# Softplus as one activation, down products split on GpSimd, three banks for up products: a two-layer kernel on one core

## The chip, the cores and the metric

The kernel runs on one core of a Trainium2 chip. The metric is device time in microseconds (us) for one execution. Engines are named as in the profile: PE (TensorE matrix products), PEld (its weight loads), DVE (VectorE), ACT (ScalarE), POOL (GpSimd), SP (SyncE, which only issues DMAs here).

## What is computed

The input is 32 sequences of 256 rows of 128 channels. Two layers follow each other, each of the form x + s(x̂) * silu(f(x̂)), where x̂ is the row-normalised x. The change touches the second layer, cut here to what matters:

```python
# s: a selective scan
xr = x @ W_in;  x_in, res = xr[..., :256], xr[..., 256:]
xc = silu(depthwise_causal_conv4(x_in) + conv_b)
p = xc @ W_x
delta = softplus(p[..., :16] @ W_dt + b_dt)        # log(1 + exp(.))
h = h * d_t + B_t * x_t;  y_t = h.sum(axis=1) * C_t
s = (y * silu(res)) @ W_out
# f: experts, 2 shared and 16 routed, 64 wide each
shared = gelu(x @ up_s) @ down_s
gate = softmax(x @ router_w.T), all but the four largest set to 0
routed = (gelu(x @ up_r) * gate) @ down_r
f = shared + routed
```

The first layer is a recurrent mixing of another kind with a three-layer network of sign weights; nothing of it is changed but how its code is written out.

## The kernel before

The 8192 rows are 16 groups of 512, turned so that channels lie on the 128 partitions and the group's rows along the free dimension: nearly every tile is 128x512. All of x stays in SBUF. The first layer runs over the 16 groups, then the second. The order of work is written out by hand, one queue per engine, with semaphores between them; nothing reorders it. Each engine's body for group step n works on three groups at once: f = n (front part), m = n - 1 (scan and down products), t = n - 2 (the last product, and the sum into x). Loops over n repeat the body; in the second layer the body comes twice in the loop, since buffers alternate.

What matters in a step of the second layer:

- The 18 experts are 9 chunks of 128 (chunk 0 is shared, 1 to 8 are routed). An **up product** (`expert_in(c)`, PE, L1177) is a split product: both factors are halved into two float16 parts, and three float16 products are summed in PSUM (high x high, high x low, low x high). It goes to one of two PSUM banks by turns. ACT takes the Gelu of it (`gelu(c)`, L662).
- A routed chunk is then multiplied by the gate: chunks 1 to 3 by POOL (L444), chunks 4 to 8 by DVE (`gated`, L1046), one step later. The **down product** (`expert_out(c)`) is one float32 product per chunk; all nine are summed in one bank.
- The gate comes from the router: Exp on ACT (L692), top four on DVE (L1009 to L1025), the spread over partitions on POOL (L434), four transposes on PE (L1419) and an evacuation by ACT (`gates_out`, L599) behind the last Gelu.
- softplus is Exp on ACT (L641), a cap on DVE (L1057), Ln on ACT (L645) and a maximum with the input on DVE (L1061).
- The scan input is L1077, the scan L1087, its output product L1094, all on DVE. `output_weight` (L1068) takes the product of output weights out of PSUM and multiplies it by the residual's Silu; `low_xc` (L1073) is the low half of the convolved input.
- The convolution is six DVE instructions (L1034) on PSUM. Row statistics are L726 and L731 on DVE, the row spread L366 and L368 on POOL, the normalising L753 on DVE.
- ACT loads another set of function tables three times a step: for Silu (L707), Exp and Ln (L685), Gelu (L697).
- The group's last steps: Silu of the experts' sum (`ffn_silu`, L604) on ACT, its product with the scan's output on DVE (L1104), transposes, and the sum into x (L1150).

## Time and profile before

| | us |
|---|---|
| median of 3 runs | 686.22 (683.71 to 689.05) |
| the profiled execution | 683.87 |
| its span, first to last instruction | 682.1 |
| PE busy | 630.9 (93%) |
| DVE busy | 630.7 (92%) |
| ACT busy | 506.7 (74%) |
| POOL busy | 280.0 (41%) |

The span is what lies between the first and the last instruction; 1.8 us lie around it. The first layer takes some 270 us of it, the second the rest. The granted clock of PE is 1.00 in every slice (2.4 GHz), but for the last at 0.96. DMA is idle but for the weights at the start and a load or store of 256 KB per group. Names: many tiles of the second layer are cut from one buffer and appear as `arena`; the PSUM banks appear as `bank`. One float32 product of 512 columns is two records. A record's length has a part that overlaps the next instruction, so the sum over a row of instructions goes by their starts. Instructions on the same line of a helper are told apart by their tiles.

### The profile page before, as it was taken

The numbers are of one execution on the slowest core, as the hardware profiler recorded it, in microseconds if no ns is written. First come the engines' busy times: TensorE is split into PE (matmuls) and PEld (weight loads), VectorE is DVE, ScalarE is ACT, GpSimd is POOL, SyncE is SP. The second block draws the span as 40 slices with busy tenths as digits, with TensorE's granted clock in tenths as the row PEclk, the third lists the DMA queues.
The fourth block names the chain that finished last, engine by engine and source line by source line (L and its number), as shares of the span: only waits on it lengthen the run. The fifth ranks groups of instructions, "written<-read, shape, count | busy, mean of one in ns | idle before, by whom it ended". The sixth has DMA issues, their size and how long they took to land. (4 is left out here: it accounts for less than half of the span.)

```text
span 682.1 us, 10868 instructions
## 1 busy us (share of the span) xinstructions
PE 630.9 (93%) x2714; PEld 301.5 (44%) x2714; DVE 630.7 (92%) x1470; ACT 506.7 (74%) x808; POOL 280.0 (41%) x275
## 2 busy tenths in 40 slices
PE   4779999999999997889999999999999999999985
PEld 2334444444444443444444444444444444444442
DVE  4999999999999999989999999999999999999866
ACT  2846666666666665887887888888789788888874
POOL 6557777777676765133122212303303221230220
PEclk9999999999999999999999999999999999999999
DMA  7331000000000000000000000000000000000000
GB/s 174 106 94 31 0 1 0 0 0 0 0 0 0 0 0 0 1 1 0 17 17 0 16 15 0 16 15 0 15 15 15 0 15 15 0 15 15 0 16 31
DMA packets 10739, 11.29 MB, mean 17 GB/s; under 512 B 4800, under 2 KB 6288, under 8 KB 10720
## 3 DMA queue, kind: packets, MB, share of 16 engines
q1 hardware_dynamic: 9744, 10.73, 5.3%
q0 software_dynamic: 112, 0.33, 0.1%
q8 instruction: 8, 0.13, 0.1%
q10 hardware_dynamic: 864, 0.00, 0.1%
q14 instruction: 11, 0.09, 0.0%
HBM read 6.87 MB, written 4.19 MB: 16 GB/s over the span
## 5 line engine op out<-in xcount | busy, mean ns | idle before, releaser
L1177 PE MATMUL bank<-arena,w 128*128 128x512 f16 x640 | 148.6, 379 | 4.0 <-DVE arena L788 4.0
L1177 PE MATMUL bank<-arena,dnT 128*128 128x512 f32 x288 | 138.6, 592 | 0.0
L662 ACT ACTIVATE arena<-bank,xinv 128x512 f32<-128x512 f32 x144 | 94.8, 688 | 37.7 <-PE bank L1177 37.5
L444 POOL TENSOR_TENSOR arena<-arena 128x512 f32<-128x512 f32 x48 | 59.7, 1273 | 135.5 <-ACT arena L599 135.5
L1177 PEld LDWEIGHTS bank<-arena,w 128*128 128x128 f16 x640 | 62.5, 98 | 78.2 <-issue 10.0
L491 ACT ACTIVATE arena<-bank 128x512 f16<-128x512 f32 x96 | 53.9, 607 | 35.6 <-PE bank L1177 35.6
L434 POOL TENSOR_TENSOR arena<-arena 128x512 f32<-128x512 f32 x16 | 16.8, 1051 | 151.6 <-DVE arena L1025 151.6
L1177 PEld LDWEIGHTS bank<-arena,dnT 128*128 128x128 f32 x288 | 53.7, 191 | 35.9 <-issue 21.2
L1177 PE MATMUL bank<-arena,wsqT 128*128 128x512 f32 x128 | 64.5, 608 | 4.7 <-DVE arena L797 4.7
L1034 DVE SCALAR_TENSOR_TENSOR arena<-bank,cws,arena 128x506 f32<-128x506 f32 (+1 forms) x96 | 67.0, 740 | 1.1
L788 DVE SCALAR_TENSOR_TENSOR arena<-bank,arena 128x512 f16<-128x512 f32 x96 | 60.2, 670 | 2.4 <-ACT arena L491 1.2
L1046 DVE TENSOR_TENSOR arena<-arena 128x512 f32<-128x512 f32 x80 | 52.3, 686 | 0.0
L409 POOL TENSOR_TENSOR arena<-arena 128x512 f16<-128x512 f32 x32 | 36.9, 1156 | 18.0 <-ACT arena L491 18.0
L413 POOL TENSOR_TENSOR arena<-arena 128x512 f32<-128x512 f32 x16 | 20.3, 1271 | 48.1 <-DVE arena L835 45.2
L488 ACT ACTIVATE arena<-bank 128x512 f32<-128x512 f32 x32 | 19.1, 597 | 27.1 <-PE bank L1177 27.1
L1087 DVE TENSOR_TENSOR_SCAN arena<-arena 128x256 f32<-128x256 f32 x64 | 38.9, 668 | 0.0
L368 POOL TENSOR_TENSOR rstd<-ve,neghalf 128x4 f32<-128x4 f32 x32 | 37.2, 1164 | 2.5
L1177 PE MATMUL bank<-arena,wcH 128*128 128x512 f16 x128 | 38.1, 379 | 0.0
L637 ACT ACTIVATE arena<-arena 128x512 f32<-128x512 f32 x32 | 20.2, 631 | 18.8 <-DVE arena L1034 18.8
L1177 PEld LDWEIGHTS bank<-arena,wsqT 128*128 128x128 f32 x128 | 24.6, 195 | 21.5 <-issue 9.1
L1177 PE MATMUL bank<-xh,upH 128*128 128x512 f16 x72 | 27.3, 380 | 6.3 <-ACT arena L662 4.6
L1177 PE MATMUL bank<-arena,w_out 128*128 128x512 f32 x64 | 30.2, 594 | 3.1 <-DVE arena L1094 3.1
(223 smaller groups left out, 1497.7 us busy)
## 6 DMA issues: line engine op xcount, KB each, us to landing
x_all<-in_L_attn_x SPq DMA_DIRECT2D x16, 256.0 KB, 2.6
out<-x_all SPq DMA_DIRECT2D x16, 256.0 KB, 2.0
up_n<-in_L_ffn_routed_up SPq DMA_DIRECT2D x1, 512.0 KB, 4.0
dn_n<-in_L_ffn_routed_down SPq DMA_DIRECT2D x1, 512.0 KB, 5.6
wx<-in_L_attn_W_x SPq DMA_DIRECT2D x1, 288.0 KB, 2.8
k_u<-in_L_ffn_k POOLq DMA_DIRECT2D x1, 256.0 KB, 5.7
w_in<-in_L_attn_W_in SPq DMA_DIRECT2D x1, 256.0 KB, 2.7
k_u<-in_L_ffn_k SPq DMA_DIRECT2D x1, 128.0 KB, 6.6
```

The source lines that it names most:

```text
L368: g.tensor_tensor(rstd[:, :], ve[:, :], neghalf[:, :], ALU.pow).then_inc(sem[ph + "rstd"], 1)
L409: g.tensor_tensor(hl[:, 1, j, :], relu[:, j, :], hh[:, 1, j, :], ALU.subtract).then_inc(sem["a_low"], 1)
L413: g.tensor_tensor(ya[:, :], ysr[:, :], rec[:, :], ALU.mult).then_inc(sem["a_y"], 1)
L444: g.tensor_tensor(prod[:, c, :], act[:, c + 1, :], gate[:, :], ALU.mult).then_inc(sem["b_actp"], 1)
L491: a.activation(hh[:, layer, j, :], src, ACT.Relu).then_inc(sem[("a_hi0", "a_hi1")[layer]], 1)
L637: a.activation(xc[:, par, k, :], u[:, k, :], ACT.Silu).then_inc(sem["b_xc"], 1)
L662: a.activation(act[:, c, :], q_U[(c + 1) % 2][:, :], ACT.Gelu, scale=xinv[:, I_UP:I_UP + 1]).then_inc(sem["b_act"], 1)
L788: v.scalar_tensor_tensor(hl[:, layer, j, :], b_Z[layer][j][:, :], 0.0, hh[:, layer, j, :], ALU.max, ALU.subtract).then_inc(sem[("a_lo0", " ...
L1034: v.scalar_tensor_tensor(uk, seqs(q_U[k][:, :])[:, :, 0:T - back], cws[:, k, t:t + 1], uk, ALU.mult, ALU.add)\
L1046: v.tensor_tensor(prod[:, c, :], act[:, c + 1, :], gate[:, :], ALU.mult).then_inc(sem["b_actg"], 1)
L1087: last = v.tensor_tensor_scan(H[:, k, w], delta[:, k, w], bx[:, k, w], 0.0, ALU.mult, ALU.add)
L1177: return nc.tensor.matmul(ps, lhsT, rhs, start=start, stop=stop)
```

## The change

It does these things:

- softplus becomes one ACT instruction with a table set of its own; ACT's order is now Exp set, router Exp, `high_xc(0)`, softplus set, two Softplus, Gelu set. The caps and maxima on DVE are gone.
- POOL takes chunks 1 to 4 instead of 1 to 3, and makes two float16 halves of each gated product: product, rounding, subtraction. It does them in two pairs: chunks 1 and 2 at the end of its step, right behind the gate, chunks 3 and 4 in the next step behind the row spread. DVE multiplies four chunks instead of five.
- The down products of chunks 1 to 4 are split: three float16 products instead of one float32. Weights are scaled and split once, at the start (`down_out`), which needs one more maximum of magnitudes.
- Up products of all groups but the first go to three banks by turns (`q_E`), the third being a bank that the output weights use before; the first of them therefore waits for `b_cr`, the end of the second output weight. PE's order of down products changes.
- The gate is transposed behind the fourth up product (before: the sixth) and evacuated behind the fifth Gelu (before: the ninth).
- All loops are written out.

```diff
-    GP = 3
+    GP = 4
...
+        q_E = (q_D[0], q_U[0], q_U[1])
...
+        def up_bank(n, c):
+            return q_U[(c + 1) % 2] if n == 0 else q_E[c % 3]
...
         def paired(eng, body):
-            for n in range(3):
-                body(n, n % 2)
-            with eng.Fori(0, (G - 4) // 2) as i:
-                body(2 * i + 3, 1)
-                body(2 * i + 4, 0)
-            for n in range(G - 1, G + 2):
+            for n in range(G + 2):
                 body(n, n % 2)
...
+            def gated_halves(m, c):
+                def product(c):
+                    pool.wait_ge(sem["b_act"], UC * m + c + 2)
+                    if not c % 2:
+                        after(pool, sem["b_down"], UC * m if c else UC * (m - 1) + 3)
+                    pool.wait_ge(sem["b_gate"], m + 1)
+                    if c % 2:
+                        pool.wait_ge(sem["b_p"], GP * m + c)
+                    g.tensor_tensor(pp[:, c % 2, :], act[:, c + 1, :], gate[:, :], ALU.mult).then_inc(sem["b_p"], 1)
+                def high(c):
+                    g.tensor_scalar(ph[:, c, :], pp[:, c % 2, :], 1.0, None, ALU.mult).then_inc(sem["b_ph"], 1)
+                def low(c):
+                    pool.wait_ge(sem["b_ph"], GP * m + c + 1)
+                    if not c % 2:
+                        pool.wait_ge(sem["b_p"], GP * m + c + 2)
+                    g.tensor_tensor(pl[:, c, :], pp[:, c % 2, :], ph[:, c, :], ALU.subtract).then_inc(sem["b_actp"], 1)
+                product(c)
+                product(c + 1)
+                high(c)
+                low(c)
+                high(c + 1)
+                low(c + 1)
...
             def layer1(n):
                 f, m = n, n - 1
-                if has(m):
-                    for c in range(GP):
-                        pool.wait_ge(sem["b_act"], UC * m + c + 2)
-                        after(pool, sem["b_down"], UC * m)
-                        pool.wait_ge(sem["b_gate"], m + 1)
-                        g.tensor_tensor(prod[:, c, :], act[:, c + 1, :], gate[:, :], ALU.mult).then_inc(sem["b_actp"], 1)
                 if has(f) and has(f + 1):
                     spread_of_rows(f + 1, "b_")
+                if has(m):
+                    gated_halves(m, 2)
                 if has(f):
                     spread_gates(f)
+                    gated_halves(f, 0)
...
-                def exponential(k):
...
-                def logarithm(k):
...
+                def softplus(k):
                     actv.wait_ge(sem["b_xdt"], IC * m + k + 1)
+                    after(actv, sem["b_scan"], IC * m)
+                    a.activation(delta[:, k, :], xdt[:, k, :], ACT.Softplus).then_inc(sem["b_delta"], 1)
...
                         if c == 5 and has(f + 1):
                             turned_high(f + 1, 1 - par, q_D[1])
-                    gates_out()
+                        if c == 4:
+                            gates_out()
...
                     gated(GP + 2)
-                    cap(0)
-                    cap(1)
                     output_weight(1)
...
                     gated(GP + 3)
-                    gated(GP + 4)
-                    softplus(0)
-                    softplus(1)
                     state(0)
...
-            DOWN_BEHIND = {1: 5, 3: 6, 6: 7, 7: 8}
+            DOWN_BEHIND = {0: 4, 5: 7, 7: 8}
...
                 def low_rank():
                     after(pe, sem["b_cr"], IC * m)
+                    if m != 0:
+                        pe.wait_ge(sem["b_act"], UC * m + UC - 2)
...
+                    elif c >= 3:
+                        pe.wait_ge(sem["b_act"], UC * f + c - 2)
+                    elif c:
+                        pe.wait_ge(sem["b_conv"], IC * f * (TAPS - 1) + CONV_DONE[c - 1])
                     else:
-                        pe.wait_ge(sem["b_conv"], IC * f * (TAPS - 1) + CONV_DONE[1 - c])
+                        pe.wait_ge(sem["b_cr"], IC * m + IC)
...
+                    if 0 < c <= GP:
+                        mm(q_F[:, :], dnH[:, w], ph[:, c - 1, :], False, False)
+                        mm(q_F[:, :], dnH[:, w], pl[:, c - 1, :], False, False)
+                        last = mm(q_F[:, :], dnL[:, w], ph[:, c - 1, :], False, False)
...
                     expert_out(2)
+                    expert_out(5)
                     expert_out(3)
-                    expert_out(4)
+                    expert_out(6)
...
-                    if has(f) and c == 5:
+                    if has(f) and c == 3:
                         gates_turned()
```

POOL's queue over one steady step, from one gate spread to the next, before; L444 is the gated product of chunks 1 to 3, L366 and L368 the row spread, L434 the gate spread:

```order
L434 TENSOR_TENSOR arena<-arena 128x512
L444 TENSOR_TENSOR arena<-arena 128x512 x3
L366 TENSOR_TENSOR ve<-mv,epsc 128x4
L368 TENSOR_TENSOR rstd<-ve,neghalf 128x4
L434 TENSOR_TENSOR arena<-arena 128x512
```

And now, from gate spread (L432) to gate spread; L444 is a product, L447 a rounding, L453 a subtraction, L364 and L366 the row spread:

```order
L432 TENSOR_TENSOR arena<-arena 128x512
L444 TENSOR_TENSOR arena<-arena 128x512 x2
L447 TENSOR_SCALAR arena<-arena 128x512
L453 TENSOR_TENSOR arena<-arena 128x512
L447 TENSOR_SCALAR arena<-arena 128x512
L453 TENSOR_TENSOR arena<-arena 128x512
L364 TENSOR_TENSOR ve<-mv,epsc 128x4
L366 TENSOR_TENSOR rstd<-ve,neghalf 128x4
L444 TENSOR_TENSOR arena<-arena 128x512 x2
L447 TENSOR_SCALAR arena<-arena 128x512
L453 TENSOR_TENSOR arena<-arena 128x512
```

Three wide instructions became twelve (the last rounding and subtraction of the second pair are cut off above), one half ahead of the row spread and one behind it.

ACT's queue from the second convolution Silu to the first Gelu, before (L641 Exp, L692 router Exp, L651 `high_xc`, L645 Ln):

```order
L637 ACTIVATE arena<-arena 128x512 x2
L685 ACT_TABLE_LOAD
L641 ACTIVATE arena<-arena 128x512 x2
L692 ACTIVATE pe_<-arena,xinv 128x4x16
L651 ACTIVATE arena<-arena,fac 128x512
L645 ACTIVATE arena<-arena 128x512 x2
L697 ACT_TABLE_LOAD
```

And now (L708 router Exp, L670 `high_xc`, L664 Softplus):

```order
L659 ACTIVATE arena<-arena 128x512 x2
L704 ACT_TABLE_LOAD
L708 ACTIVATE pe_<-arena,xinv 128x4x16
L670 ACTIVATE arena<-arena,fac 128x512
L710 ACT_TABLE_LOAD
L664 ACTIVATE arena<-arena 128x512 x2
L714 ACT_TABLE_LOAD
```

Four activations became two, and a third table load stands between the Silu and the Gelu.

PE's queue from the product for the scan input (s2B) on, before; bank7 sums the down products, banks 4 and 5 take the up products, dnT is a float32 down weight:

```order
L1177 MATMUL bank0<-arena,s2B 128x512
L1177 MATMUL bank7<-arena,dnT 128x512 x3
L1177 MATMUL bank5<-xh_,upH 128x512
L1177 MATMUL bank5<-xl_,upH 128x512
L1177 MATMUL bank5<-xh_,upL 128x512
```

And now; the up products go to banks 2, 4 and 5 by turns, dnH and dnL are the halves of down weights:

```order
L1194 MATMUL bank0<-arena,s2B 128x512
L1194 MATMUL bank7<-arena,dnH 128x512 x2
L1194 MATMUL bank7<-arena,dnL 128x512
L1194 MATMUL bank7<-arena,dnT 128x512
L1194 MATMUL bank7<-arena,dnH 128x512 x2
L1194 MATMUL bank7<-arena,dnL 128x512
L1194 MATMUL bank7<-arena,dnT 128x512
L1194 MATMUL bank2<-xh_,upH 128x512
L1194 MATMUL bank2<-xl_,upH 128x512
L1194 MATMUL bank2<-xh_,upL 128x512
```

Three float32 down products have become two split ones (three matmuls each) and two float32 ones, and the first up product behind them goes to bank2, not to bank5.

## Rows read from the trace of the kernel before

**Rows 1.** Windows of one step each: bounds, length, busy time by engine, granted clock, DMA share, GB/s.

```profile
476.98:501.46 24.48, 23.92 (x104) 11.48 (x104) 23.06 (x62) 20.50 (x32) 5.98 (x6) 1.00 0.03 11
501.46:525.84 24.38, 23.86 (x104) 11.50 (x104) 23.06 (x62) 20.49 (x32) 5.99 (x6) 1.00 0.03 11
```

**Rows 2.** PE's timeline inside one step: start, length, engine, line, operation, tiles, form, count, wait.

```profile
500.78 0.60 PE L1188 MATMUL bank<-ident,xn 128*128 128x128 f32 x4
501.94 0.39 PE L1177 MATMUL bank<-xh_,upH 128*128 128x512 f16 x1 [0.56 <-ACT arena L662]
...
506.49 1.02 PE L1177 MATMUL bank<-arena,dnT 128*128 128x512 f32 x2
507.34 0.38 PE L1177 MATMUL bank<-xh_,upH 128*128 128x512 f16 x1
507.56 0.38 PE L1177 MATMUL bank<-xl_,upH 128*128 128x512 f16 x1
```

**Rows 3.** DVE's timeline inside one step, same columns.

```profile
488.50 0.69 DVE L1104 TENSOR_TENSOR sg<-bank,gp 128x512 f32<-128x512 f32 x1 [1.04 <-ACT gp L604]
...
490.60 4.26 DVE L1034 SCALAR_TENSOR_TENSOR arena<-bank,cws,arena 128x506 f32<-128x506 f32 x6
494.78 1.11 DVE L753 TENSOR_SCALAR xn<-x_all,mv,rstd 128x128 f32 x4
...
498.27 0.76 DVE L1057 TENSOR_SCALAR arena<-arena 128x512 f32<-128x512 f32 x2
498.94 0.75 DVE L1068 SCALAR_TENSOR_TENSOR arena<-bank,fac,arena 128x512 f32<-128x512 f32 x1
...
503.22 1.28 DVE L1046 TENSOR_TENSOR arena<-arena 128x512 f32<-128x512 f32 x2
504.42 1.28 DVE L1061 TENSOR_TENSOR arena<-arena 128x512 f32<-128x512 f32 x2
505.62 2.43 DVE L1087 TENSOR_TENSOR_SCAN arena<-arena 128x256 f32<-128x256 f32 x4
...
512.89 0.69 DVE L1104 TENSOR_TENSOR sg<-bank,gp 128x512 f32<-128x512 f32 x1 [0.95 <-ACT gp L604]
```

**Rows 4.** ACT's timeline inside one step.

```profile
485.89 0.59 ACT L599 ACTIVATE arena<-bank 128x512 f32<-128x512 f32 x1
...
494.90 0.63 ACT L637 ACTIVATE arena<-arena 128x512 f32<-128x512 f32 x1 [0.81 <-DVE arena L1034]
...
496.85 1.15 ACT L641 ACTIVATE arena<-arena 128x512 f32<-128x512 f32 x2
...
501.20 1.27 ACT L662 ACTIVATE arena<-bank,xinv 128x512 f32<-128x512 f32 x2
```

**Rows 5.** POOL's timeline inside one step.

```profile
486.64 3.73 POOL L444 TENSOR_TENSOR arena<-arena 128x512 f32<-128x512 f32 x3 [8.62 <-ACT arena L599]
...
490.94 1.01 POOL L368 TENSOR_TENSOR rstd<-ve,neghalf 128x4 f32<-128x4 f32 x1
```

**Rows 6.** Timeline of three stretches in which DVE and POOL work side by side.

```profile
255.65 2.19 DVE L850 TENSOR_TENSOR_SCAN Pv<-dec,arena 128x256 f32<-128x256 f32 x2
255.88 1.42 POOL L419 TENSOR_TENSOR arena<-arena,Pk 128x512 f32<-128x512 f32 x1 [1.31 <-DVE Pk L841]
...
264.80 2.26 POOL L409 TENSOR_TENSOR arena<-arena 128x512 f16<-128x512 f32 x2
265.52 2.13 DVE L753 TENSOR_SCALAR xn<-x_all,mv,rstd 128x128 f32<-128x128 f32 x4
...
659.69 1.26 POOL L444 TENSOR_TENSOR arena<-arena 128x512 f32<-128x512 f32 x1
659.74 0.68 DVE L1051 SCALAR_TENSOR_TENSOR arena<-bank,arena 32x512 f16<-32x512 f32 x1
660.46 1.65 DVE L1046 TENSOR_TENSOR arena<-arena 128x512 f32<-128x512 f32 x2
```

**Rows 7.** Groups by line and form, POOL: the one small conversion to float16.

```profile
L402 POOL TENSOR_SCALAR w<-k_u 128x512 f16<-128x512 uint8 x1 | 0.6, 615 | 0.0
```

More of the change, by code:

```diff
@@ L292, in peeled @@
                     between[n]()
-            for n in range(3):
-                peeled(n)
-            with eng.Fori(3, G - 1) as n:
-                body(n)
-            for n in range(G - 1, last):
+            for n in range(last):
                 peeled(n)
         def paired(eng, body):
-            for n in range(3):
-                body(n, n % 2)
-            with eng.Fori(0, (G - 4) // 2) as i:
-                body(2 * i + 3, 1)
-                body(2 * i + 4, 0)
-            for n in range(G - 1, G + 2):
+            for n in range(G + 2):
                 body(n, n % 2)
@@ L524, in layer0 @@
                     high(1, m, 2)
-                if isinstance(f, int) and f == 0:
+                if f == 0:
                     for j in range(FC):
@@ L539, in layer0 @@
                     a.activation(thr[:, :], b_RX[:, :], ACT.Tanh, scale=0.5).then_inc(sem["a_thr"], 1)
-                    if not (isinstance(f, int) and f == 0):
+                    if f != 0:
                         high(0, f, 0)
@@ L544, in layer0 @@
                     a.activation(sr[:, :], thr[:, :], ACT.Copy, scale=0.5, bias=0.5).then_inc(sem["a_sr"], 1)
-                    if not (isinstance(f, int) and f == 0):
+                    if f != 0:
                         high(0, f, 1)
@@ L597, in gates_out @@
                     after(actv, sem["b_actg"], GV * f)
-                    after(actv, sem["b_actp"], GP * f)
-                    a.activation(gate[:, :], q_Q[:, :], ACT.Copy).then_inc(sem["b_gate"], 1)
+                    after(actv, sem["b_p"], GP * f)
+                    a.activation(gate[:, :], q_Q[:, :], ACT.Copy, scale=down[:, GATE_S:GATE_S + 1]).then_inc(sem["b_gate"], 1)
                 def ffn_silu():
@@ L603, in ffn_silu @@
                     after(actv, sem["b_sg"], t)
-                    a.activation(gp[:, :], q_F[:, :], ACT.Silu).then_inc(sem["b_g"], 1)
+                    a.activation(gp[:, :], q_F[:, :], ACT.Silu, scale=down[:, SUM_S:SUM_S + 1]).then_inc(sem["b_g"], 1)
                 def conv_input(k):
@@ L678, in layer1 @@
                     res_silu(1)
-                if isinstance(n, int) and n == 0:
+                if n == 0:
                     up_high(2)
@@ L807, in layer0 @@
                         dve.wait_ge(sem["bn_done"], f + 2)
-                    if not (isinstance(f, int) and f == 0):
+                    if f != 0:
                         dve.wait_ge(sem["a_z0"], FC * f)
@@ L852, in layer0 @@
                     last.then_inc(sem["a_scanV"], 1)
-                if has(f) and not (isinstance(f, int) and f == 0):
+                if has(f) and f != 0:
                     low(0, f, 0)
@@ L955, in down_out @@
                 dve.wait_ge(sem["prep_turned"], UB + i + 1)
-                v.tensor_copy(dnT[:, i * WB * P:(i + 1) * WB * P], q_W[UB + i][:, 0:WB * P]).then_inc(sem["prep_out"], 1)
+                at = i * WB * P
+                full = [c for c in range(i * WB, (i + 1) * WB) if c == 0 or c > GP]
+                split = [c for c in range(i * WB, (i + 1) * WB) if 0 < c <= GP]
+                for c in full:
+                    at_c = max(0, c - GP) * P
+                    last = v.tensor_scalar(dnT[:, at_c:at_c + P], q_W[UB + i][:, c * P - at:(c + 1) * P - at],
+                                           col(down, SHARED_S) if c == 0 else col(wsc, I_DN), None, ALU.mult)
+                if split:
+                    w = slice((split[0] - 1) * P, split[-1] * P)
+                    last = halves(dnH[:, w], dnL[:, w], q_W[UB + i][:, w.start + P - at:w.stop + P - at], col(wsc, I_DN))
+                last.then_inc(sem["prep_out"], 1)
             def turned_low(n, par=0, ps=q_T):
@@ L1125, in layer1 @@
                         conv(f, k, tap)
-                if isinstance(n, int) and n == 0:
+                if n == 0:
                     up_low(2)
@@ L1143, in layer1 @@
                     gates(f)
-                if isinstance(n, int) and n == 0:
+                if n == 0:
                     matrices()
@@ L1447, in layer1 @@
                     residual_in(1)
-                if isinstance(n, int) and n == 0:
+                if n == 0:
                     turn_weights(2)
```

139 lines of the change are left out of this document (70 added, 69 removed).

## Prediction

> **What bounds the kernel now.** I read the windows of one group of the second layer first, then the timeline of each engine inside one group, and last the places where VectorE and GpSimd work at the same moment. Both bounds of each window are starts of GpSimd's L434, so the window is one group's period: 24.48 and 24.38 us [rows 1]. There are 15 such intervals between the first and the last of the 16 groups, 363 us of the span; the first layer holds most of the rest and is changed only by losing its loops. In the window PE is busy 23.9 of 24.4 us, DVE 23.1, ACT 20.5, POOL 6.0 [rows 1]: two engines are near the limit, one is far from it.
>
> PE's timeline shows how its work is priced. A split product of 512 columns takes a step of 0.216 us (507.34 to 507.56), so three of them 0.65; one float32 product is two records and takes 0.85 (506.49 to 507.34) [rows 2]. PE has one gap of note in the group, 0.56 us before the third expert product (L662, Gelu), which I count as 0.73 against the steady step: the four transposes before it start at 500.78 in steps of 0.11, so 0.44, and the next product starts at 501.94 [rows 2]. What uses a product may start 0.17 after its step (a record of 0.38 less the step). DVE's timeline is a closed row of work from L1104 on: its one idle stretch is 0.95 to 1.04 us before L1104, where it waits for the Silu behind the table load [rows 3]. So PE's pure work is 24.43 - 0.73 = 23.7 us a group and DVE's 24.43 - 1.0 = 23.4.
>
> **What goes.** PE: four float32 down products (0.85) become three float16 ones (0.65) each: 4 x 0.21 = 0.85 us less, 22.85 a group. DVE: two caps from 498.27 to 498.94 (0.67), two maxima from 504.42 to 505.62 (1.20), and one of five gated products (0.60, half the step of 503.22 to 504.42): 2.47 us less, 20.95 [rows 3]. ACT: two Exp and two Ln at some 0.53 become two Softplus, for which I take the same 0.53 (two Exp 1.15 with the last one's end, a Silu 0.63 [rows 4]; bounds 0.5 to 0.7), and one table load is added, 1.32 us from the Silu's end (495.53) to the first Exp (496.85) [rows 4]. That is +0.25 us, ACT 20.75 of a period of 23 or more: below the limit. The new load lies between the last convolution Silu and the first Gelu: 6.30 us now (494.90 to 501.20 [rows 4]), then 6.30 - 4 x 0.53 + 2 x 0.53 + 1.32 = 6.6. The third bank lets PE do three expert products before it needs that Gelu, which covers it. The Trainium skill (ScalarE: Activation LUTs, What ACT_TABLE_LOAD costs) gives about 2.66 us for every switch of sets; by it ACT would gain 1.6 us a group and still not be the limit. The rows show 1.32, and I keep to them. The loops: the two intervals differ by 0.10 [rows 1], at most 0.1 per jump and 0.6 us in all; I take 0.3.
>
> With nothing added, PE would set 22.85 us a group: 15 x 1.58 = 24 us less.
>
> **What is added, and what it meets.** GpSimd now does per group four products, four roundings to float16 and four subtractions. The product is 1.24 (three in 3.73 us [rows 5]). The subtraction is of the kind of L409, two in 2.26, 1.15 one [rows 6]. The rounding is not in the trace in this form; the nearest is L402, 0.62 for 512 elements [rows 7]; bounds 0.6 and 1.16, I take 0.62. With 0.08 us for each wait inside a pair, a pair is 2 x 1.26 + 2 x 0.62 + 2 x 1.15 + 0.2 = 6.3 us, two pairs 12.6; with the rest GpSimd has some 15 us. It has the time. The question is when it works.
>
> Rows 6 show three meetings. Two gated products on DVE at 660.46 take 1.65 and not 1.28 (503.22 [rows 3]): GpSimd's L444 ends at 660.95, and the first of them ends 0.55 later, at 661.50, having taken 1.05 and not 0.68. DVE's scan L850 second half starts near 256.2, L419 ends at 257.30, the scan at 257.84. Four normalising instructions L753, one input and of the fast kind, take 2.13 us beside two L409 at 265.52, and 1.11 where GpSimd rests (494.78 [rows 3]). It works the other way too: L419 takes 1.42, since the first of the two scans ends only near 256.32, and 0.98 of it follow. L1051, one of whose inputs lies in PSUM, runs beside L444 in its usual 0.68. I take this as the rule: a DVE instruction with two SBUF inputs, or of the fast one-input kind, and a wide GpSimd instruction exclude each other, and where both queues are full they alternate. Each such DVE instruction then costs its own time and the GpSimd one's: about 1.0 us for a product, 0.9 for a subtraction, 0.4 for a rounding. The Trainium skill says the same (GPSIMD Engine Reference, Key points: the SBUF interfaces are shared with VectorE, contention with DVE in a 2-port mode or with two SBUF inputs); the trace agrees, 1.05 for 0.68.
>
> Now GpSimd's three products run at 486.64 to 490.37 [rows 5], beside row statistics, PSUM readers and idle time. Both new places are worse:
>
> Pair two (chunks 3 and 4) starts behind the row spread, which ends 1.35 us after the convolution starts (490.94 + 1.01 against 490.60 [rows 3, 5]). Its products lie beside the convolution, free. Its rounding starts at +3.9; at +4.18 the convolution ends, and four L753 and two gated products meet rounding, subtraction, rounding, subtraction. Alternating, the four L753 are through at about +6.5 and not +5.2, one gated product waits for the last subtraction, and the second output weight ends at +10.5 instead of +8.4: 2.1 us (1.4 if more slip through per gap).
>
> Pair one (chunks 1 and 2 of the next group) starts with the gate. Count from E, PE's first expert product, which now waits for the second output weight, so DVE's end of it is E too. On PE six steps of 0.65 (five expert products and one down product), two sets of transposes of 0.44 and the latency of 0.17 give the fifth product at E + 4.95; the Gelu (0.69) and the evacuation of the gate (L599, 0.59 [rows 4], overlapping) end at 6.15, and GpSimd starts 0.15 later, as it does now behind L599 (486.48 and 486.64 [rows 4, 5]), at 6.3. On DVE, from E: top four to L1077's end 3.6 (498.94 + 0.67 to 503.22 [rows 3]), one gated product 4.2, four scans 6.6. Then come two output products and two L1073, all with two SBUF inputs, to 9.1. They meet product, product, rounding, subtraction: if DVE is first, 1.0 + 0.4 + 0.9 is close to 2.2 us; if GpSimd is first, 3.15. The two requests lie within 0.1 us of each other, so I keep both.
>
> **The sum.** DVE: 20.95 + 2.1 + 2.2 = 25.3, or + 3.15 = 26.2 us a group. DVE would then be at L1104 at E + 12.5 to 13.5, behind the Silu, which ends at 11.9 (ninth expert product at 9 x 0.65 + 0.65 + 2 x 0.44 + 2 x 0.85 = 9.1, latency 0.17, Gelu 0.69, load 1.3, Silu 0.6): it never waits, and it sets the period. PE's 22.85 fit below. I take 25.8: +1.37 a group, x 15 = +20.5 us. The first group has three small DVE instructions more and split weights (+1). The tail loses caps, maxima, a Ln and 0.85 us of PE, some 2 us, less a meeting there. Loops -0.3. Total +19.5 us on 683.87 (span 682.1 and 1.8 around it) is 703.4. The median shown, 686.22, is 2.35 us above that execution; I say 704.0.
>
> **Rivals.**
> A, faster: the meetings cost little, because GpSimd gives way in the gaps or the pairs slide beside the PSUM readers. For it: GpSimd has 8 us of free time a group, and DVE frees 2.47. Against it: rows 6. Then PE sets 22.85, -24 us: 661; if only pair two meets, DVE has 23.05 and the time is about 664. It decides when the two meetings cost together under 1.9 us. Chance 0.25.
> B, no change: the meetings eat what DVE gained. They cost about 3.5 us a group, 24.4: 682 to 688. That needs DVE first at pair one and L753 slipping through two per gap. Chance 0.15.
> C, the forecast: 4.3 to 5.3 us of meetings, own range 692 to 714. Chance 0.6; within it, a rounding at 1.16 us adds up to 1 us a group, 718.
> D, that the third bank does nothing: the gap of 0.73 is PE's and it is gone or moved in all cases, so it would change 661 to about 671 in A and nothing in C.
>
> The range takes the lower bound of B and most of C's dear side: 676 to 718; case A lies mostly outside. A measurement of this kernel can tell about 1% from no change. Faster by more than 1% 0.25, within 1% 0.15, slower by more than 1% 0.60.
>
> **What would show it.** Right: a period near 25.8 between GpSimd's gate spreads; no idle DVE before its Silu product; the output products and the subtractions L1073 over 1.0 us in the mean, where a gated product of that size alone takes 0.68; the four normalising instructions over 0.5; PE waiting for the second output weight and for the output products; three-bank Gelus with no gap behind the table load. Wrong: DVE instruction lengths as before (then A, and PE would show no gap), a GpSimd rounding far from 0.62, or a Softplus that is not as long as an Exp.

## The result, and the profile after

The change makes the kernel slower: 697.50 us (696.64 to 699.95, median of 4 runs) against 685.76 (683.71 to 689.05, a fourth run beside the three of the table ahead), ratio 1.0172, 95% interval [1.0123, 1.0222]. The forecast was 704.0, with a range of 676 to 718.

The page of the changed kernel, its first part:

```profile
span 694.8 us, 9584 instructions
PE 624.9 (90%) x2778; PEld 294.6 (42%) x2778; DVE 649.0 (93%) x1399; ACT 518.1 (75%) x796; POOL 499.5 (72%) x419
```

PE lost 6 us of busy time. DVE should have lost some 39 (16 groups of 2.47) and gained 18: it is the engine that was to be relieved, and its meetings with GpSimd lengthened its instructions by more than was taken away. POOL went from 280 to 500. One step by windows, bounded by starts of the gate spread as in [rows 1] (length, then busy time of PE, PEld, DVE, ACT, POOL, granted clock, DMA share, GB/s):

```profile
487.22:512.51 25.29, 23.46 (x109) 11.08 (x109) 24.26 (x57) 21.04 (x30) 19.48 (x15) 1.00 0.03 11
```

25.29 us against 24.48 and 24.38. Over the whole second layer the 15 intervals are read from the gate spread's line, whose first and last starts are given (before: 283.75 to 647.10, mean 24.22):

```profile
L432 POOL TENSOR_TENSOR arena<-arena x16: 1038/1039/1214, 283.7 to 662.1; 128x512 f32<-128x512 f32 x16
```

The mean is 25.23, +1.0 a group, 15 us; the tail behind the last spread is 2.3 us shorter, and the two make the 12.7 us by which the span grew. Of the 15 us the first interval alone has 4.8 (27.27 against 22.44), the other fourteen 10.2.

POOL's timeline in that step shows each instruction (L444 product, L447 rounding, L453 subtraction, L364 and L366 row spread):

```profile
492.87 1.45 POOL L444 TENSOR_TENSOR arena<-arena 128x512 f32<-128x512 f32 x1 [4.61 <-ACT arena L621]
494.78 1.27 POOL L444 TENSOR_TENSOR arena<-arena 128x512 f32<-128x512 f32 x1 [0.46 <-ACT arena L681]
496.01 1.93 POOL L447 TENSOR_SCALAR arena<-arena 128x512 f16<-128x512 f32 x1
498.02 1.16 POOL L453 TENSOR_TENSOR arena<-arena 128x512 f16<-128x512 f32 x1
499.14 1.49 POOL L447 TENSOR_SCALAR arena<-arena 128x512 f16<-128x512 f32 x1
500.72 1.16 POOL L453 TENSOR_TENSOR arena<-arena 128x512 f16<-128x512 f32 x1
...
502.11 1.04 POOL L366 TENSOR_TENSOR rstd<-ve,neghalf 128x4 f32<-128x4 f32 x1
503.12 1.27 POOL L444 TENSOR_TENSOR arena<-arena 128x512 f32<-128x512 f32 x1
504.56 1.27 POOL L444 TENSOR_TENSOR arena<-arena 128x512 f32<-128x512 f32 x1 [0.17 <-POOL arena L444]
505.80 1.50 POOL L447 TENSOR_SCALAR arena<-arena 128x512 f16<-128x512 f32 x1
507.38 1.84 POOL L453 TENSOR_TENSOR arena<-arena 128x512 f16<-128x512 f32 x1
509.20 1.92 POOL L447 TENSOR_SCALAR arena<-arena 128x512 f16<-128x512 f32 x1
511.20 1.15 POOL L453 TENSOR_TENSOR arena<-arena 128x512 f16<-128x512 f32 x1
```

From 492.87 to 512.35 POOL is idle for no more than 0.46 us at a time. The rounding takes 1.49 at least and 1.93 where it meets VectorE; the prediction had 0.62. And DVE beside it, to be laid against [rows 3]:

```profile
493.11 3.48 DVE L1095 SCALAR_TENSOR_TENSOR arena<-arena,fac 128x512 f16<-128x512 f32 x2
...
498.46 0.69 DVE L1126 TENSOR_TENSOR sg<-bank,gp 128x512 f32<-128x512 f32 x1 [0.49 <-ACT gp L626]
...
504.90 2.48 DVE L771 TENSOR_SCALAR xn<-x_all,mv,rstd 128x128 f32<-128x128 f32 x4
...
508.80 0.97 DVE L1077 TENSOR_TENSOR arena<-arena 128x512 f32<-128x512 f32 x1
...
511.90 0.53 DVE L1056 TENSOR_TENSOR arena<-pe_,arena 128x64 f32<-128x64 f32 x1
```

The two low_xc (L1095) take 3.48 (1.40 where GpSimd rests, a_late below), four normalisings (L771) 2.48 for 1.11, one gated product (L1077) 0.97 for 0.68, and the subtraction that closes the gates (L1056) 0.53 for 0.22. VectorE's product behind the experts' Silu (L1126) still waits 0.49 us, so the engine is not closed. PE's waits in the step name both engines:

```profile
507.67 1.12 PE L1194 MATMUL bank<-arena,dnT 128*128 128x512 f32 x2 [0.54 <-DVE arena L1077]
509.28 0.60 PE L1194 MATMUL bank<-arena,dnH 128*128 128x512 f16 x2 [0.49 <-POOL arena L453]
...
512.41 0.60 PE L1194 MATMUL bank<-arena,dnH 128*128 128x512 f16 x2 [0.80 <-POOL arena L453]
```

So PE now waits 1.8 us a step; that its own work fell as forecast is measured by a_tiny below.

### The profile page after: what moved, and what is told of

Same layout as the page of the kernel before. It is cut to its first block, busy times and chain, and to the rows that moved or that the text cites. A ratio compares the mean times of both kernels' runs of the same rounds, so it can differ in the third digit from the quotient of the medians.

```text
span 694.8 us, 9584 instructions
## 1 busy us (share of the span) xinstructions
PE 624.9 (90%) x2778; PEld 294.6 (42%) x2778; DVE 649.0 (93%) x1399; ACT 518.1 (75%) x796; POOL 499.5 (72%) x419
## 4 chain that ended last, share of the span: by engine, by line
PE 29%; DVE 27%; POOL 5%; issue 4%; ACT 1%; DVEq 1%; POOLq 0%; ACTq 0%
PE bank L1194 27%; DVE arena L1065 8%; DVE arena L1077 4%; DVE xn L771 4%; DVE arena L1090 3%; POOL arena L453 3%; POOL arena L447 1%; PE bank L1205 1%; PE bank L1453 1%; DVE mv L749 1%; DVE arena L1042 1%; POOL arena L444 1%; DVE arena L806 1%; DVE arena L1134 0%; DVE arena L1048 0%
## 5 line engine op out<-in xcount | busy, mean ns | idle before, releaser
L444 POOL TENSOR_TENSOR arena<-arena 128x512 f32<-128x512 f32 x64 | 88.2, 1378 | 77.3 <-ACT arena L621 71.6
L447 POOL TENSOR_SCALAR arena<-arena 128x512 f16<-128x512 f32 x64 | 109.8, 1716 | 0.0
L1194 PE MATMUL bank<-arena,dnT 128*128 128x512 f32 x160 | 83.0, 601 | 7.2 <-DVE arena L1077 7.2
L453 POOL TENSOR_TENSOR arena<-arena 128x512 f16<-128x512 f32 x64 | 83.5, 1305 | 5.3
L1194 PE MATMUL bank<-arena,dnH 128*128 128x512 f16 x128 | 38.4, 382 | 20.0 <-POOL arena L453 20.0
L411 POOL TENSOR_TENSOR arena<-arena 128x512 f32<-128x512 f32 x16 | 20.3, 1271 | 48.3 <-DVE arena L853 45.4
L1095 DVE SCALAR_TENSOR_TENSOR arena<-arena,fac 128x512 f16<-128x512 f32 x32 | 54.1, 1729 | 0.0
L407 POOL TENSOR_TENSOR arena<-arena 128x512 f16<-128x512 f32 x32 | 36.9, 1156 | 18.1 <-ACT arena L513 18.1
L1077 DVE TENSOR_TENSOR arena<-arena 128x512 f32<-128x512 f32 x64 | 48.1, 770 | 0.0
L771 DVE TENSOR_SCALAR xn<-x_all,mv,rstd 128x128 f32<-128x128 f32 x68 | 38.4, 639 | 1.5 <-POOL rstd L366 1.5
L366 POOL TENSOR_TENSOR rstd<-ve,neghalf 128x4 f32<-128x4 f32 x32 | 37.6, 1174 | 2.5
L1194 PEld LDWEIGHTS bank<-arena,dnT 128*128 128x128 f32 x160 | 28.2, 191 | 21.9 <-DVE arena L1077 14.3
```

Of the source, the lines that this page charges most:

```text
L444: g.tensor_tensor(pp[:, c % 2, :], act[:, c + 1, :], gate[:, :], ALU.mult).then_inc(sem["b_p"], 1)
L447: g.tensor_scalar(ph[:, c, :], pp[:, c % 2, :], 1.0, None, ALU.mult).then_inc(sem["b_ph"], 1)
L453: g.tensor_tensor(pl[:, c, :], pp[:, c % 2, :], ph[:, c, :], ALU.subtract).then_inc(sem["b_actp"], 1)
L771: last = v.tensor_scalar(xn[:, j, :], x_all[:, bass.ds(n * N + j * P, P)], mv[:, j, 0:1], rstd[:, j:j + 1], ALU.subtract, ALU.mult)
L1077: v.tensor_tensor(prod[:, c - GP, :], act[:, c + 1, :], gate[:, :], ALU.mult).then_inc(sem["b_actg"], 1)
L1095: v.scalar_tensor_tensor(xcl[:, k, :], xc[:, par, k, :], fac[:, XC_S:XC_S + 1], xch[:, k, :], ALU.mult, ALU.subtract).then_inc(sem["b_xcl" ...
```

## The experiments

Two theories stood behind them. **D**, the prediction's: VectorE, lengthened by its meetings with GpSimd, sets the period. **G**, formed on the trace after: a ring through GpSimd sets it. Pair one, row spread and pair two follow each other without a gap, PE waits for the last half before its next up products, and these, the fifth Gelu and the gate's evacuation let the next pair one start. By the rows the two pairs and the spread are 19.48 us (492.87 to 512.35) and the way over PE and ScalarE back to the next pair one 5.8, together the 25.29 of the step. All ratios are to the kernel before; "us" is a median, and "period" the mean of the 15 intervals of the one profiled execution, read as above.

| run | us | ratio, 95% interval | period |
|---|---|---|---|
| before | 685.76 | | 24.22 |
| after | 697.50 | 1.0172 [1.0123, 1.0222] | 25.23 |
| u_only | 685.76 | 0.9992 [0.9974, 1.0009] | 24.12 |
| u_soft | 688.45 | 1.0032 [1.0006, 1.0059] | 24.49 |
| u_banks | 687.78 | 1.0027 [1.0008, 1.0046] | 24.49 |
| u_soft_banks | 680.96 | 0.9926 [0.9902, 0.9949] | 23.89 |
| a_tiny | 668.67 | 0.9733 [0.9691, 0.9774] | 23.31 |
| a_tiny2 | 680.39 | 0.9915 [0.9887, 0.9943] | 24.16 |
| a_ring | 693.60 | 1.0109 [1.0061, 1.0157] | 24.94 |
| a_late | 706.90 | 1.0304 [1.0270, 1.0337] | 25.71 |
| a_act_ring | 703.46 | 1.0242 [1.0199, 1.0285] | 25.50 |
| a_tt | 743.50 | 1.0833 [1.0778, 1.0888] | 28.12 |
| a_quiet | 730.24 | 1.0630 [1.0580, 1.0679] | 27.07 |
| best | 680.77 | 0.9917 [0.9888, 0.9947] | 24.04 |

### The parts alone

**u_only**: the kernel before, all loops written out.

```diff
-            with eng.Fori(0, (G - 4) // 2) as i:
-                body(2 * i + 3, 1)
-                body(2 * i + 4, 0)
+            for n in range(G + 2):
+                body(n, n % 2)
```

> The kernel before with its loops written out and nothing else. Theory of the prediction: a jump costs at most 0.1 us and there are six pairs of steps in the second layer, so 0 to -0.6 us, within 0.3% of before. Rival (written-out code is slow to fetch, and the change pays for it): some us slower, up to the whole +11.7 us of the change, with the extra spread over all engines.

0.9992 with 1 inside its interval. The loops are no part of the result.

**u_soft**: u_only with caps, maxima, Exp and Ln replaced by this.

```diff
+                a.preload_act_table_set(SOFT_SET)
+                if has(m):
+                    softplus(0)
+                    softplus(1)
```

> Loops written out and softplus as one activation with its own table set; two banks, three float32 gated products on GpSimd as before. Theory (PE sets the period, and its one gap of 0.73 us hangs on the first Gelu): ACT reaches that Gelu 0.25 us later, so the gap grows to about 1.0, +0.25 us a group, +4 us: about 690. Rival (DVE sets the period): DVE loses 1.87 us a group and the time falls by up to 15 us.

688.45, slower as forecast. The wait moved, the first row from u_only, the second from u_soft:

```profile
476.08 0.39 PE L1166 MATMUL bank<-xh,upH 128*128 128x512 f16 x1 [0.43 <-ACT arena L651]
```

```profile
483.15 0.39 PE L1147 MATMUL bank<-xh,upH 128*128 128x512 f16 x1 [0.82 <-ACT arena L647]
```

PE is busy 23.87 in both windows and the wait for the first Gelu is all that differs: +0.39 a step for one table load more. These are two single executions, of 682.80 and 691.15 us, at opposite ends of their kernels' runs; the medians differ by 2.7 us, which is 0.18 a step, so the sign is sure and the size is not. VectorE lost 1.9 us of work and spent it waiting.

**u_banks**: u_only with three banks.

```diff
+            return q_U[(c + 1) % 2] if n == 0 else q_E[c % 3]
...
+                    else:
+                        pe.wait_ge(sem["b_cr"], IC * m + IC)
```

> Loops written out and three banks for the up products; softplus and gated products as before. Theory: the gap of 0.73 us before the third up product goes, but the first up product now waits some 0.2 us for the second output weight, which still stands behind the two caps: -0.5 us a group, -8 us: about 678. Rival (the bank changes nothing, since something else is late by the same amount): within 2 us of before.

The forecast failed: 687.78, slightly slower. The wait for the Gelu is gone, and the first up product waits as long for the second output weight, which VectorE does behind its caps:

```profile
501.75 0.39 PE L1171 MATMUL bank<-xh_,upH 128*128 128x512 f16 x1 [0.82 <-DVE arena L1062]
```

**u_soft_banks**: both, which is the change without GpSimd's halves (three float32 products on GpSimd, nine float32 down products, the gate evacuated behind the ninth Gelu as before).

> The change without the GpSimd halves: loops written out, one softplus, three banks, but three float32 gated products on GpSimd, five on DVE and nine float32 down products. Theory: PE runs without the gap, 23.7 us a group, -0.73 x 15 = -11: about 675; so the halves alone would cost the change 22 us. Rival (softplus with its third table load is what costs): no faster than before.

680.96, faster, by less than half of the forecast. With the caps gone the wait for the output weight is 0.17:

```profile
476.59:500.63 24.04, 23.87 (x105) 11.50 (x104) 21.19 (x58) 20.84 (x31) 5.99 (x6) 1.00 0.03 12
```

24.04 = 23.87 + 0.17. Each part alone costs some 2 us against before, together they gain 5, and what the change has beyond them (the halves, the fourth product on GpSimd, the order of down products and the early gate) turns that into a loss: 697.5 - 681.0 = 16.5 us.

### What of the halves costs

**a_tiny**: the changed kernel, roundings and subtractions on one column from the second group on; the down products of chunks 1 to 4 then read stale halves.

```diff
-                    g.tensor_scalar(ph[:, c, :], pp[:, c % 2, :], 1.0, ...
+                    g.tensor_scalar(ph[:, c, 0:(1 if m else N)], pp[:, c % 2, 0:(1 if m else N)], 1.0, ...
```

> The changed kernel, but from the second group on GpSimd's roundings and subtractions work on one column instead of 512 (so the down products of chunks 1 to 4 take stale halves). PE's work and all waits stay. Theory (GpSimd's eight wide instructions more are the whole loss): PE sets the period; the run with all parts but the halves had 24.04 us, less 0.85 of PE gives 23.2, so about 668. Rival (the loss sits in the order of the waits, in PE's split down products or in the early gate): still over 685.

668.67. The eight wide instructions cost 29 us. With them narrow, the down products' order, the early gate and the waits cost nothing in a steady step, for PE is closed:

```profile
475.29:498.36 23.07, 23.07 (x110) 11.05 (x109) 22.55 (x57) 20.92 (x31) 10.08 (x15) 1.00 0.03 12
```

Here PE's work after the change is measured: 23.07, which is 23.87 less 0.80.

**a_tiny2**: the same for chunks 3 and 4 alone (pair two).

```diff
-                    g.tensor_scalar(ph[:, c, :], pp[:, c % 2, :], 1.0, ...
+                    g.tensor_scalar(ph[:, c, 0:(1 if m and c > 1 else N)], ...
```

> The changed kernel, but from the second group on the roundings and subtractions of chunks 3 and 4 alone (pair two) work on one column; those of chunks 1 and 2 are whole. So the down products of chunks 3 and 4 take stale halves. Theory: pair two holds VectorE for some 1.7 us (normalising 1.4, one gated product 0.3) and is 6.3 us of the ring; without it PE sets 23.1 to 23.3: 668 to 673, as without any halves. Rival (pair one costs as much as pair two): about 683.

680.39, close to the rival's 683. The theory's 668 to 673 failed. Pair two costs 17 us (697.5 to 680.4), and pair one 12 (to 668.7) once pair two is gone. VectorE is busy 23.63 of 24.16 in that window and waits nowhere for more than 0.22, so here it is the bound, with pair one's meetings in it.

### Which ring sets the period

**a_ring**: nothing removed; the down product of chunk 4 behind the fourth up product.

```diff
-            DOWN_BEHIND = {0: 4, 5: 7, 7: 8}
+            DOWN_BEHIND = {3: 4, 5: 7, 7: 8}
```

> The changed kernel with the split down product of chunk 4 issued behind the fourth up product, not the first. Nothing is removed. Theory G (a ring through GpSimd sets the period: pair one 9.0 us, row spread 1.25, pair two 9.2, then PE's wait for its last half, the next up products, Gelu and gate evacuation 5.8): the ring loses PE's wait and VectorE, at some 24.8 a group, takes over: -0.5 us a group, about 690. Theory D of the prediction (VectorE alone sets the period): no change, 697.

693.60, 4 us less than after, and no run of either reaches the other's (692.08 to 695.18 against 696.64 to 699.95). D has no change here. VectorE's wait before L1126 is gone and the engine is closed:

```profile
485.14:510.21 25.07, 23.46 (x110) 11.06 (x108) 24.54 (x57) 21.12 (x31) 20.25 (x16) 1.00 0.04 12
```

24.54 busy of 25.07: cutting the ring gave back 0.3 a step in the mean, and in this step VectorE is the bound, as D has it. The gain is small because VectorE's busy time rose from 24.26 to 24.54. Pair one starts earlier, so it runs into the two output products too, in some steps; by the groups of lines (steps of 400 to 640 us; busy, mean ns) they have 992 where the changed kernel has 669:

```profile
L1116 DVE TENSOR_TENSOR arena<-arena 128x512 f32<-128x512 f32 x20 | 19.1, 992 | 0.0
```

**a_late**: one wait more, none removed.

```diff
+                    if not c:
+                        pool.wait_ge(sem["b_xcl"], IC * m + IC)
```

> The changed kernel with one wait more: GpSimd starts the products of chunks 1 and 2 only behind VectorE's second low_xc, so that the two low_xc (3.48 us beside GpSimd) take their own 1.41 again. Theory D (VectorE sets the period): VectorE has 2.1 us less, 22.7, and PE at 23.5 with its waits takes over: 680 or less. Theory G (the ring through GpSimd sets it): pair one starts 1.8 us later and takes 8.0 instead of 9.0, so the ring is 0.8 us longer: +12, about 709.

706.90, near G's 709. Under D this run would have been far faster, for VectorE is relieved:

```profile
491.93:517.68 25.75, 23.46 (x109) 11.08 (x109) 22.66 (x57) 21.05 (x30) 18.42 (x15) 1.00 0.03 11
```

and waits 2.57 us before its experts' product:

```profile
497.82 1.40 DVE L1097 SCALAR_TENSOR_TENSOR arena<-arena,fac 128x512 f16<-128x512 f32 x2
...
503.18 0.69 DVE L1128 TENSOR_TENSOR sg<-bank,gp 128x512 f32<-128x512 f32 x1 [2.57 <-ACT gp L628]
```

VectorE loses 1.6 us of work a step and the kernel loses 9 us against after. So VectorE by itself does not set the period. The run alone doesn't show that G's ring did so before the wait was added: GpSimd now starts behind low_xc (it waits 6.42 us for L1097), and with that the ring passes through VectorE too. With a_ring, where nothing was removed and the time fell, and with the 0.49 us that VectorE waits in the changed kernel, it does follow: there the ring through GpSimd is the bound, and VectorE lies 0.3 to 0.5 us a step below it.

### The rule of the meetings

**a_tt**: the rounding as a second gated product, written in float16.

```diff
-                    g.tensor_scalar(ph[:, c, :], pp[:, c % 2, :], 1.0, None, ALU.mult)...
+                    g.tensor_tensor(ph[:, c, :], act[:, c + 1, :], gate[:, :], ALU.mult)...
```

> The changed kernel with GpSimd's rounding written as the gated product once more, into float16: 1.15 us by the trace for that kind of instruction, where the rounding takes 1.50 to 1.93. Theory G (ring through GpSimd): the ring loses 4 x 0.35 to 0.7, some 2 us, and VectorE at 24.8 takes over, about 690. Theory D: VectorE meets an instruction with two inputs where it met one with one input, so no change or up to 1 us a group more: 697 to 710.

743.50, far beyond either. POOL did get faster (17.7 us busy a step, each rounding 1.26 to 1.29), but the four normalisings take 4.06:

```profile
533.51 4.06 DVE L771 TENSOR_SCALAR xn<-x_all,mv,rstd 128x128 f32<-128x128 f32 x4
537.49 2.24 DVE L1077 TENSOR_TENSOR arena<-arena 128x512 f32<-128x512 f32 x2
```

```profile
533.76 1.27 POOL L447 TENSOR_TENSOR arena<-arena 128x512 f16<-128x512 f32 x1
535.11 1.16 POOL L453 TENSOR_TENSOR arena<-arena 128x512 f16<-128x512 f32 x1
536.22 1.26 POOL L447 TENSOR_TENSOR arena<-arena 128x512 f16<-128x512 f32 x1
537.57 1.62 POOL L453 TENSOR_TENSOR arena<-arena 128x512 f16<-128x512 f32 x1
```

The last three of the four (1.31, 1.31 and 1.30 long) end with POOL's L447, L453 and L447 in turn: one passes per POOL instruction, the alternation of the prediction. In the changed kernel the second, third and fourth all started while the one-input rounding of 505.80 was under way, and the gated product behind them started at 506.93: 1.1 us by the starts, where three alone take 0.8. So in these rows a one-input GpSimd instruction lets VectorE's one-input instructions pass with a small delay, and a two-input one holds each of them. A part of this run's loss is PE's clock (last section).

**a_act_ring**: the roundings on ScalarE, and a_ring's order of down products.

```diff
-                high(c)
                 low(c)
-                high(c + 1)
                 low(c + 1)
...
+                    a.activation(ph[:, c, :], pp[:, c % 2, :], ACT.Copy).then_inc(sem["b_ph"], 1)
```

> The changed kernel with the four roundings on ScalarE (0.6 us each, 2.4 a group: 21.0 + 2.4 = 23.4) and the down product of chunk 4 behind the fourth up product. GpSimd keeps products and subtractions, some 10 us. Both theories: the meetings with VectorE fall from 3.7 us to about 2, so VectorE has 22.6 of work; PE or ACT sets the period at 23.2 to 23.6: 668 to 675. Rival: the roundings delay the first Gelu or the experts' Silu, and ScalarE becomes the bound: over 685.

The forecast of 668 to 675 failed, at 703.46, and not by the rival's way: ScalarE is busy 22.80 of 25.35. Without roundings the products and subtractions follow more closely, and VectorE finds fewer places to pass:

```profile
510.89 2.89 DVE L779 TENSOR_SCALAR xn<-x_all,mv,rstd 128x128 f32<-128x128 f32 x4
513.70 1.28 DVE L1085 TENSOR_TENSOR arena<-arena 128x512 f32<-128x512 f32 x2
514.90 0.74 DVE L1098 SCALAR_TENSOR_TENSOR arena<-bank,fac,arena 128x512 f32<-128x512 f32 x1
515.56 1.16 DVE L1085 TENSOR_TENSOR arena<-arena 128x512 f32<-128x512 f32 x1
```

VectorE is busy 24.89, more than with the roundings on GpSimd. GpSimd lost 6 us of busy time a step and none of what hurts.

**a_quiet**: a_late, the row spread inside pair one, chunks 3 and 4 behind the first and fourth up products.

```diff
                 high(c)
+                if c == 0 and has(m + 2):
+                    spread_of_rows(m + 2, "b_")
...
+            DOWN_BEHIND = {0: 3, 3: 4, 5: 7, 7: 8}
```

> a_late, and the ring cut: the row spread stands inside pair one (behind its first rounding) instead of between the pairs, and the down product of chunk 3 stands behind the first up product, that of chunk 4 behind the fourth. Same work everywhere. Both theories: pair one lies beside VectorE's PSUM readers, VectorE has some 22.7 and GpSimd some 18.5 in no ring, PE sets 23.0 to 23.4 a group: 668 to 676. Rival: GpSimd, fed too late, is still waited for by VectorE's normalising or by PE: over 690.

730.24, the rival's side and worse. GpSimd waited 1.98 us for the row moments; with that the rest of pair one and both products of pair two slid beside the normalisings:

```profile
520.64 3.79 DVE L775 TENSOR_SCALAR xn<-x_all,mv,rstd 128x128 f32<-128x128 f32 x4
524.35 1.72 DVE L1081 TENSOR_TENSOR arena<-arena 128x512 f32<-128x512 f32 x2
```

They take 3.79, the first gated product behind them comes late, PE waits 2.23 us for it, and then runs at half its clock in this step (last section).

### A version from it

**best**: three products on GpSimd and five on VectorE, chunks 1 and 2 split alone, GpSimd behind the second low_xc.

```diff
+                product(0)
+                product(1)
+                product(2)
...
+                high(0)
+                low(0)
+                if has(m + 2):
+                    spread_of_rows(m + 2, "b_")
+                high(1)
+                low(1)
```

> The parts that gained (one softplus, three banks, early gate), three gated products on GpSimd and five on VectorE, and only chunks 1 and 2 split. GpSimd starts behind VectorE's second low_xc: three products, rounding and subtraction of chunk 1, the row spread, rounding and subtraction of chunk 2, all beside VectorE's row statistics and convolution; down products in the order of before. Theory: VectorE has 21.2 + 0.4 of meetings + 0.4, some 22, GpSimd is in no ring, PE has 23.87 - 0.42 and a wait of 0.1: 23.55 a group against the 24.04 of the run without halves, so 681 - 7 = 674, faster than both kernels. Rival: the last subtraction meets the normalising, GpSimd feeds rstd late, and PE idles again: 681 or more.

680.77: 0.9917 of before and 2.4% under the changed kernel's time, but the same as u_soft_banks, and the forecast of 674 failed. The halves are hidden as meant: VectorE is busy 21.59, one normalising of four is held 0.4. The wait for the second output weight took the gain:

```profile
476.66:500.86 24.20, 23.45 (x107) 11.42 (x106) 21.59 (x58) 21.01 (x31) 11.21 (x11) 1.00 0.03 12
```

```profile
499.14 0.39 PE L1197 MATMUL bank<-xh_,upH 128*128 128x512 f16 x1 [0.75 <-DVE arena L1092]
```

23.45 + 0.75 = 24.20. PE's work fell by 0.42, as worked out, and the wait rose from 0.17 to 0.75. It seems to close a ring of its own: first up product, ninth Gelu, Silu of the experts, VectorE's product behind it (which waits 2.07 us here), convolution, output weights, first up product. By the rows it is 13.1 us on PE and ScalarE (474.94, one period ahead of the row above, to 488.02) and 11.1 on VectorE (to 499.14). The two split down products stand ahead of the first up product and so outside it, the four behind are as they were; the waits are read from the trace, but the ring is argued and not shown: no run cut it, and a reordering of those four was not tried.

## Why the prediction was right, and where it was not

**The direction and the place of the loss were right.** The added GpSimd work meets VectorE at the two places that were named, and the time rose. Removing that work alone (a_tiny) takes 29 us off; the one softplus and the third bank together gain 5.

**The meetings, term by term.** Lengths of records overlap, so this goes by starts. Pair two was put at 2.1 us: measured are 1.0 on the normalisings (504.90 to 506.93 against 494.78 to 495.81), 0.3 on a gated product and 0.3 on the gates' subtraction, 1.6. Pair one was put at 2.2 or 3.15: measured are 2.1, all on the two low_xc, and none on the output products, which had passed before GpSimd started. Together 3.7 against 4.3 to 5.3. Sound as far as it goes; VectorE has 20.95 + 3.7 = 24.65, where the trace shows 25.29 with one wait of 0.49 in it, 24.8.

**The signs that were named.** Borne out: low_xc over 1.0 in the mean (1.76), the normalisings over 0.5 (0.67), no gap behind the table load, a Softplus as long as an Exp (two in 1.15). Not borne out: VectorE waits before its Silu product, the output products keep their 0.67, and PE waits in the steady step neither for the second output weight nor for the output products, but for GpSimd's halves and one gated product. And one sign of being wrong came: a rounding far from 0.62.

**The step that failed: "It has the time", with the rounding at 0.62.** The row taken was one that reads bytes, and the upper bound of 1.16, from the float32 subtraction, was still too low. The rounding is 1.49 to 1.93, four of them 6.8 us instead of 2.5. GpSimd is busy 19.5 of 25.3 and not 15, and with the waits between its pairs it closes a ring that the prediction did not have. a_ring and a_late together show that this ring bounds the changed kernel, with VectorE right behind it. The time of 704 came from 25.8 a group, the measured steady one is 25.26. That it came so near is luck in part: two errors of opposite sign, a VectorE term 1.0 us too long and a ring that was missing and adds 0.5.

**The first interval** was put at +1 us beyond a steady step's +1.4 and is +4.8. In the first step of the layer VectorE makes the split weights (some 1.2 us more ahead of its low_xc), the low_xc meet GpSimd (2.60 us for 1.41), and PE rests for the down weights behind them, after which it is granted half its clock for a while (last section). VectorE's convolution so starts 4.2 us later, counted from the first gate spread. Behind it the normalisings and two gated products cost 1.3 more, and the caps that are gone give back 0.7. The tail was put at -2 and is -2.3. By the terms: fourteen intervals 10.2 where 19.2 were forecast, the first 4.8 where some 2.4 were, and the tail as forecast.

**PE's share.** "4 x 0.21 = 0.85 less" is 0.80 (a_tiny). But its pure work was 23.87 and not 23.7, since the gap before the third up product was counted as 0.73 and is 0.43 to 0.56. That made PE's floor 23.07 and not 22.85, some 3 us over 15 groups of the 7.7 by which a_tiny's 668.7 lies above rival A's 661; the rest is mostly a_tiny's first interval, 28.09.

**Rival D** was dismissed too soon: that the third bank gives nothing by itself is what u_banks shows. It was called a gain in all cases but C; in truth it trades the wait for the Gelu for one for the second output weight, and pays only where the caps are gone. ACT's part was right in kind: one load more is +0.25 by the sum, and +0.39 in the profiled execution of u_soft or 0.18 by its median, of no account where PE doesn't wait for that Gelu. The 2.66 us of the Trainium skill for a switch of sets (ScalarE: Activation LUTs, What ACT_TABLE_LOAD costs) would have made it some 1.6; the measured step bears out the 1.3 of the rows.

**Rival A** had its price almost right and its condition wrong. VectorE does get through in one case, that of one-input instructions on both sides, which is why the normalisings came off with 2.48; a_tt shows 4.06 where it does not.

## What to carry to other kernels

Work moved to an engine that was 41% busy was not free here, since its instructions shut out those of an engine near the limit. Before moving, list which instructions of that engine will stand beside it, and count each that has two operands in SBUF with the time of one foreign instruction (here 1.0 us for a low_xc behind a product). Making the mover faster, or shortening its queue, doesn't help by itself (a_tt, a_act_ring): what counts is what each of its instructions stands beside.

A buffer added to remove one wait brings the wait for whoever frees that buffer; read which step does and when (u_banks). Two edits that each cost 2 us can gain 5 together, so single-part runs alone don't decide.

A chain of small delays on an idle-looking engine can close into a ring over two steps. Two tests go together: an edit that cuts the ring and removes no work (a_ring), and a delay on that engine that relieves the other one (a_late). If the second makes the time longer, the relieved engine alone was not the bound.

## What the runs showed of the hardware

**Which pairs hold each other.** A VectorE instruction with two SBUF inputs behind a GpSimd product ends some 0.55 later than it: the two low_xc of 493.11 end at 496.59, the second product beside them at 496.05. One takes 1.76 in the mean instead of 0.7. With one input on each side they pass with a small delay: 2.48 for four normalisings, where two-input GpSimd instructions all along give 4.06. The page of the Trainium skill that the prediction cites (GPSIMD Engine Reference, Key points) has the first case; the trace agrees, and the second is what a_tt against the changed kernel adds.

**GpSimd's rounding of float32 to float16 (one input, 128x512) takes 1.49 alone**, the float16 subtraction with two inputs 1.16. The one-input form is the slower one.

**PE's clock after an idle stretch.** In a_quiet PE rests from 523.3 to 525.5 and is then granted 0.50, 1.2 GHz, until about 528.5; by windows of 1 us, columns as above:

```profile
524.00:525.00 1.00, 0.00 (x0) 0.00 (x0) 1.00 (x2) 0.99 (x2) 1.00 (x2) 1.00 0.00 0
525.00:526.00 1.00, 0.48 (x1) 0.48 (x2) 1.00 (x3) 1.00 (x2) 0.92 (x2) 0.72 0.00 0
526.00:527.00 1.00, 1.00 (x2) 0.36 (x2) 1.00 (x3) 0.98 (x2) 1.00 (x1) 0.50 0.00 0
527.00:528.00 1.00, 1.00 (x2) 0.34 (x1) 1.00 (x2) 0.42 (x1) 1.00 (x2) 0.50 0.00 0
```

Two float32 products take 3.62 us there; in the changed kernel's window two such take 1.88 (495.54). a_tt has the same behind a wait of 2.49. So in these steps a wait costs its length and 1.5 to 2 us more, which no forecast had; it is a part of why these two runs came out so dear. The changed kernel has it too, in the first step of the layer, where four products on s1W take 1.87 us instead of 1.02:

```profile
294.54 1.87 PE L1194 MATMUL bank<-arena,s1W 128*128 128x512 f16 x4 [2.96 <-DVE dnT L982]
```

```profile
295.00:296.00 1.00, 1.00 (x4) 0.36 (x3) 0.21 (x2) 0.00 (x0) 1.00 (x1) 0.50 0.00 0
```

The length of the rest alone doesn't decide. The waits of 0.80 in the changed kernel's step and of 1.36 in a_act_ring leave the clock at 1.00, but so does one of 1.93 at the same place in the kernel before (first row) and one of 2.70 in a_late (second row), which is longer than that in a_quiet. What does decide is not shown by these runs.

```profile
291.79 1.02 PE L1177 MATMUL bank<-arena,s1W 128*128 128x512 f16 x4 [1.93 <-DVE dnT L956]
```

```profile
307.03 1.12 PE L1196 MATMUL bank<-arena,dnT 128*128 128x512 f32 x2 [2.70 <-DVE arena L1079]
```
